# Loading, masking and releasing the attention bias of a head in two halves

## The reference, cut to what matters

```python
scores = einsum('bhqd,bhkd->bhqk', q / sqrt(16), k)      # 8 batches, 16 heads, 512 x 512
scores = scores + attention_bias                         # fp32, 1 MB for one head of one batch
scores = where(src_mask, -inf, scores)                   # the mask is the same for all heads of a batch
probs  = softmax(scores)
ctx    = einsum('bhqk,bhkd->bhqd', probs, v)
```

## Time and profile before

| | |
|---|---|
| time, median of 3 runs | 1041.93 us (1038.78 to 1044.15) |
| profiled execution, span | 1036.6 us (5.3 us under the median; its whole time is not recorded) |
| attention block | first `add_bias` at 39.8 us, last at 706.7 us of the span |
| one batch in the middle | 83.9 to 84.1 us |
| busy over the span | PE 92%, DVE 78%, ACT 71%, POOL 70% |
| bias loads | 128 of 1024 KB, median 8.0 us from issue to landing |

### The profile page before, as it was taken

The page is one execution under the profiler, slowest core; times in us unless marked ns, Lnnn a source line. Parts: engine busy times, 40 slices in busy tenths (PEclk is TensorE's granted clock), DMA queues, the critical chain, the costliest instruction groups (busy, mean ns, idle before and its releaser), DMA issues. The chain is left out here.

```text
span 1036.6 us, 20438 instructions
## 1 busy us (share of the span) xinstructions
PE 956.1 (92%) x5892; PEld 640.9 (62%) x5892; DVE 813.7 (78%) x2075; ACT 734.7 (71%) x1211; POOL 726.3 (70%) x596
## 2 busy tenths in 40 slices
PE   5879999999999999999999999898999999999963
PEld 4646556656655655755665665454777777777752
DVE  8887797878879879879787887874456877887697
ACT  3577887888798788788788878875446556655433
POOL 3487697788788878878778878777555567755631
PEclk9989999999999999999999999999999999999987
DMA  7978978997996997897799799752111111111001
GB/s 262 334 289 292 381 289 278 363 347 238 346 384 214 336 386 257 291 390 292 265 372 343 237 348 370 252 193 82 41 41 41 42 33 50 42 41 41 21 21 41
DMA packets 127535, 230.33 MB, mean 222 GB/s; under 512 B 5488, under 2 KB 53872, under 8 KB 123632
## 3 DMA queue, kind: packets, MB, share of 16 engines
q1 hardware_dynamic: 127472, 229.60, 62.0%
HBM read 187.63 MB, written 41.94 MB: 221 GB/s over the span
## 5 line engine op out<-in xcount | busy, mean ns | idle before, releaser
L937 ACT ACTIVATE prob<-prob,nmax 128x512 f32<-128x512 f32 x512 | 357.0, 729 | 59.6 <-DVE nmax L762 56.4
L762 DVE CUSTOM_DVE_ANT_0 prob<-s_bank,big 128x512 f32<-128x512 f32 x512 | 338.7, 684 | 69.7 <-POOL big L1101 40.3
L1101 POOL TENSOR_TENSOR big<-big,mterm_early 128x2048 f32<-128x2048 f32 (+2 forms) x88 | 305.3, 3484 | 71.5 <-DMA big<-in_fside_Bx16xSxS 62.3
L593 PEld LDWEIGHTS t_bank<-ident,prob 128*128 128x128 f32 x2048 | 238.1, 141 | 168.3 <-issue 51.5
L593 PE MATMUL t_bank<-ident,prob 128*128 128x128 f32 x2048 | 317.7, 278 | 15.9 <-ACT prob L937 6.7
L944 ACT COPY pt<-t_bank 128x512 f32<-128x512 f32 x312 | 181.1, 584 | 51.7 <-PE t_bank L593 50.6
L581 PE MATMUL s_bank<-stack_k,stack_q 128*128 128x512 bf16 x512 | 195.4, 382 | 1.3 <-DVE nmax L762 0.7
L771 DVE COPY pt<-t_bank 128x512 f32<-128x512 f32 x200 | 137.2, 686 | 34.9 <-PE t_bank L593 34.6
L2052 POOL TENSOR_TENSOR gl<-big,gh 128x512 fp32r<-128x512 f32 x64 | 84.6, 1329 | 69.8 <-DVE gh L1643 69.8
L607 PE MATMUL o_bank<-pt,val 128*32 128x512 f32 x1024 | 122.9, 598 | 1.2 <-ACT pt L944 0.7
L1905 ACT ACTIVATE big<-bank,late 128x512 f32<-128x512 f32 x62 | 42.7, 689 | 75.2 <-PE bank L1446 71.4
(11 more groups left out here) (257 smaller groups left out, 1610.0 us busy)
## 6 DMA issues: line engine op xcount, KB each, us to landing
big<-in_fside_Bx16xSxS SPq DMA_DIRECT2D x128, 1024.0 KB, 8.0
pieces_dram<-pieces SPq DMA_DIRECT2D x64, 384.0 KB, 7.3
stack_q<-pieces_dram SPq DMA_DIRECT2D x15, 1024.0 KB, 8.3
stack_k<-pieces_dram SPq DMA_DIRECT2D x15, 1024.0 KB, 10.0
pieces_dram<-pieces SPq DMA_DIRECT2D x32, 256.0 KB, 7.6
xin<-in_x SPq DMA_DIRECT2D x8, 512.0 KB, 8.7
x_dram<-x SPq DMA_DIRECT2D x8, 512.0 KB, 2.6
x1r<-x_dram SPq DMA_DIRECT2D x8, 512.0 KB, 4.3
```

The source lines that it names most:

```text
L593: last = pe.transpose(t_bank[n % 2][:, c * P:(c + 1) * P], prob[:, n % NT, c * P:(c + 1) * P], ident[:])
L762: dve.tensor_tensor_reduce(out=prob[:, n % NT, :], in0=s_bank[n % 3][:, :], in1=bias[:, h % NB, t, :], scale=-1.0, scalar=3e38, op0=ALU.ad ...
L937: act.activation(tile, tile, ACT.Exp, bias=nmax[:, n % NT:n % NT + 1], scale=-1.0).then_inc(exped.sem, 1)
L1101: pool.tensor_tensor(bias[:, h % NB, tiles], bias[:, h % NB, tiles], mterm[:, tiles], ALU.add).then_inc(masked.sem, 1)
```

## The change

Three things:

1. The four tiles of a bias buffer are two halves of two tiles. Each half has a semaphore of its own for its load, is loaded by a DMA of its own (512 KB, 256 runs of 2 KB), is masked by an instruction of its own (two instructions of 1024 elements in place of one of 2048; 1024 and 512 for head 4) and is released by itself: SP waits for `biased` of tiles 0 and 1, loads the first half of head h + 4, waits for tiles 2 and 3, loads the second half.
2. DVE waits at tiles 0 and 2, each time for its half.
3. All `apart` increments of all engines and both blocks go to one semaphore.

The core of the diff (all other lines replace the name of a spacing semaphore, or count halves where heads were counted):

```diff
+HALF = QT // 2
+POOL_HALVES = [(h, i) for h in POOL_HEADS for i in range(2) if POOL_TILES[h] > HALF * i]
+def half_of(i):
+    return slice(HALF * i, HALF * (i + 1))
-        bias_in = [sem(f"bias_in{i}") for i in range(NB)]
+        bias_in = [[sem(f"bias_in{i}{half}") for half in range(2)] for i in range(NB)]
-        first_loads += [(bias[:, h], v["bias"][:, h], bias_in[h]) for h in range(NB)]
+        first_loads += [(bias[:, h, half_of(i)], v["bias"][:, h, half_of(i)], bias_in[h][i]) for h in range(NB) for i in range(2)]
-            def load_bias(b, h):
-                sp.dma_start(bias[:, h % NB], bias_flat[:, bass.ds(b * H + h, 1)].rearrange("p o t k -> p (o t) k")
-                             ).then_inc(bias_in[h % NB], 16)
+            def load_bias(b, h, i):
+                sp.dma_start(bias[:, h % NB, half_of(i)],
+                             bias_flat[:, bass.ds(b * H + h, 1), half_of(i)].rearrange("p o t k -> p (o t) k")
+                             ).then_inc(bias_in[h % NB][i], 16)
                 for h in range(H):
-                    if not (last and h + NB >= H):
-                        sp.wait_ge(biased.sem, biased.at(b, QT * (h + 1)))
-                        apart(sp, sp_apart)
-                        load_bias(b, h + NB)
+                    for i in range(2):
+                        if not (last and h + NB >= H):
+                            sp.wait_ge(biased.sem, biased.at(b, QT * h + HALF * (i + 1)))
+                            apart(sp, k["apart"])
+                            load_bias(b, h + NB, i)
             def add_bias(b, n):
                 h, t = n // QT, n % QT
-                if t == 0 and POOL_TILES[h]:
-                    dve.wait_ge(masked.sem, masked.at(b, POOL_HEADS.index(h) + 1))
-                elif t == 0:
-                    dve.wait_ge(bias_in[h % NB], b * (16 * H // NB) + 16 * (h // NB + 1))
+                i = t // HALF
+                if t % HALF == 0 and (h, i) in POOL_HALVES:
+                    dve.wait_ge(masked.sem, masked.at(b, POOL_HALVES.index((h, i)) + 1))
+                elif t % HALF == 0:
+                    dve.wait_ge(bias_in[h % NB][i], b * (16 * H // NB) + 16 * (h // NB + 1))
             def mask_bias(b, h):
-                pool.wait_ge(bias_in[h % NB], b * (16 * H // NB) + 16 * (h // NB + 1))
...
-                apart(pool, pool_apart)
                 mterm = mterm_early if h < EARLY_HEADS else mterm_late
-                tiles = slice(0, POOL_TILES[h])
-                pool.tensor_tensor(bias[:, h % NB, tiles], bias[:, h % NB, tiles], mterm[:, tiles], ALU.add
-                                   ).then_inc(masked.sem, 1)
+                for i in range(2):
+                    if (h, i) in POOL_HALVES:
+                        pool.wait_ge(bias_in[h % NB][i], b * (16 * H // NB) + 16 * (h // NB + 1))
+                        apart(pool, k["apart"])
+                        tiles = slice(HALF * i, min(HALF * (i + 1), POOL_TILES[h]))
+                        pool.tensor_tensor(bias[:, h % NB, tiles], bias[:, h % NB, tiles], mterm[:, tiles], ALU.add
+                                           ).then_inc(masked.sem, 1)
```

More of the change, by code:

```diff
@@ L350, in attention_block @@
         late_term = Count(sem("late_term"), QT, 0)
-        masked = Count(sem("masked"), len(POOL_HEADS), 0)
+        masked = Count(sem("masked"), len(POOL_HALVES), 0)
         res_done = Count(sem("res_done"), 1, 1)
@@ L1075, in early_mask_term @@
                     if t == 0:
-                        pool.wait_ge(masked.sem, masked.at(b, sum(h < EARLY_HEADS for h in POOL_HEADS)))
-                apart(pool, pool_apart)
+                        pool.wait_ge(masked.sem, masked.at(b, sum(h < EARLY_HEADS for h, _ in POOL_HALVES)))
+                apart(pool, k["apart"])
                 pool.tensor_scalar(
@@ L1084, in late_mask_term @@
                     pool.wait_ge(scored.sem, scored.at(b - 1, STEPS))
-                    pool.wait_ge(masked.sem, masked.at(b - 1, len(POOL_HEADS)))
-                apart(pool, pool_apart)
+                    pool.wait_ge(masked.sem, masked.at(b - 1, len(POOL_HALVES)))
+                apart(pool, k["apart"])
                 pool.tensor_scalar(
@@ L1700, in statistics @@
                 wait(dve, bn_done[i], j, 1)
-                apart(dve, dve_apart)
+                apart(dve, k["apart"])
                 for t in range(QT):
@@ L2160, in build @@
             k[n] = nc.alloc_sbuf_tensor_at(n, [P] + shape, dt, offset=at)
-        for n in ("first_in", "w1_made", "w2_made", "x1_last", "first_made", "mix_step"):
+        for n in ("first_in", "w1_made", "w2_made", "x1_last", "first_made", "mix_step", "apart"):
             k[n] = ctx.enter_context(nc.semaphore(n))
```

17 lines of the change are left out of this document (6 added, 11 removed).

## The result

The changed kernel takes 1050.72 us (median of 4 runs, 1048.93 to 1050.8), the kernel before beside it 1040.77. The ratio is 1.0093, with a 95% interval of 1.0073 to 1.0113: **0.9% slower**, where 0.7% faster was predicted. The profiled executions differ by more than the medians, 1048.7 us of span against 1036.6. (The changed file has 7 or more lines ahead of each place: `add_bias` is now L770, the normalisation L809, the low parts of xt L817, the masks L1111, PE's "XT" L636, "Q" and "K" L644, "W" L669.)

What follows compares the result with a forecast made beforehand. PE was taken to bound the attention block, busy 81.08 of a middle batch's 83.90 us. Gains of 2.8 + 4.8 = 7.6 us off 1041.9 gave 1034.3 us, 0.7% less, range 1027 to 1042.

Steps and rivals of the forecast that it cites:

- The stall is covered by PE's burst: DVE's stall for POOL's masks at head 1: PE fills it with a 1.92 us burst, so first-order gain is nothing.
- Term 1: ACT's copy of "C" before PE's "W": about 0.4 us sooner in 7 batches, 2.8 us, 0 to 5.3.
- Term 2: DVE's normalisation shares less time with POOL's late mask terms: 0.8 us in 6 batches, 4.8 us, 0 to 7.7.
- What the change adds: Extra POOL instructions, SP issues, DVE waits and the single semaphore: 1.4 us of POOL per batch, nothing in the sum.
- Rival C: Bias loads: halves land later, so POOL's masks and late terms slide over the normalisation; 1055 us for 3 us later, chance 0.12.
- Rival A: Stall covered by PE's burst and normalisation still meeting POOL: gain 0 to 5 us, typically 2.8, 1039 us; chance 0.33.
- DVE's wait under 12 us: Sign in the profile after: DVE's whole wait for POOL's masks falls from 40.3 to under 12 us.
- L801 at about 1.9: Sign: the four normalisation instructions on DVE take about 1.9 us in batches 1 to 6, against 2.66 in batch 4.
- PE's wait before "XT" about 0.5 in a batch: Sign: PE's wait for the normalised x falls to about 0.5 us, from 1.25 in batch 4.
- Before "W" 0.35: Sign: PE's wait for the copy of "C" falls to about 0.35 us, from 0.76 in batch 4.
- A batch at 82.6 to 82.8: Sign: a middle batch takes 82.6 to 82.8 us, against 83.90 before.
- It is wrong if PE's gaps move elsewhere: Condition for failure: PE's gaps move to the exponent or a copy of the steps 12 to 16; no size given.

Runs made afterwards that it cites:

- stall given back: Kernel with both waits, but DVE waits at a head's first tile for both half masks, loads and masks still in halves: 1030.93 us, ratio 0.9901.
- both waits: Changed kernel, POOL waiting for DVE's low parts of xt before head 8's masks (all batches but the last) and before the last batch's weight split: 1031.08 us.

## Why the prediction was wrong, point by point

**The stall is covered by PE's burst: right.** The changed kernel is level with before at step 8, and the 10 us of stall given back cost nothing that shows. All but about 0.2 us in a batch was free.

**Term 1, the copy of "C" 0.4 us sooner: wrong, it is 0** (within its bounds of 0 to 5.3). ACT and PE of the changed kernel, as the earlier trace rows:

```profile
387.41 0.59 ACT L952 COPY pt<-t_bank 128x512 f32<-128x512 f32 x1 [1.12 <-PE t_bank L600]
...
392.09 0.60 PE L664 MATMUL spare<-ident,con 128*128 128x128 f32 x4
...
393.35 0.62 ACT L984 COPY cont<-spare 128x512 f32<-128x512 f32 x1
394.10 1.12 PE L669 MATMUL spare<-cont,wo 128*128 128x512 f32 x2 [0.76 <-ACT cont L984]
```

ACT did lose its idle 1.33 us before the exponent, but spent the lead waiting 1.12 us for a transpose of PE, behind the burst. From the end of "C" (392.69) to its copy are 0.66 us, exactly as before (389.89 to 390.55). The failed reading is that ACT's queue was replayed with fixed durations and without the work of PE that it waits for. A lead of one engine is lost here at the first thing that it needs from another.

**Term 2, the normalisation freed of the late terms: right in mechanism, too small.** 0.8 us was taken; it was the full 1.28 of the bound in batches 1 and 3 to 6 of the changed kernel (1.38 us each, 2.05 in batch 2). The mis-sized piece is how much sooner the late terms start. The prediction took 1.2 to 2.0 us, from a mask of head 5 that still waits for its second half. In the changed kernel's batch 4 that half had landed, the four half masks before the late terms run without a gap, and the late terms start 18.60 us after the batch's first `add_bias` in place of 21.81, 3.2 us sooner. What the term is worth shows where nothing collides: with both waits batch 4 is 1.45 us under the 83.90 of before, 1.28 of it the normalisation and about 0.2 the stall. The whole sum was 7.6 us; the kernel with both waits has 9.7 by the medians and 7.6 by the profiled spans.

**"What the change adds": the step that failed.** The cost of POOL's masks was taken from their number and length, set against POOL's idle time, and the only reader thought of was DVE's `add_bias`. That POOL also *starts earlier* was used for the normalisation, where it helps, and for nothing else. The low parts, 10 us further on, were never costed: a term put at nothing without a reason. Yet the earlier trace rows held the mechanism, and the idle 2.61 us of POOL at 409.99 was in the same timeline. The new term is 1.9 us in each of batches 1 to 6, 0.5 to 1.7 in batch 0, and 7.5 in the last. With it the sum is 1034.3 + 6 x 1.9 + 7.5 and those 0.5 to 1.7, 1053.7 to 1054.9, against the 1050.7 measured; term 1, which came to nothing, is 2.8 of the difference.

The Trainium skill has this rule in the section that the prediction cited for the other line (SBUF — State Buffer, Who interferes with whom): a DVE instruction with two SBUF inputs contends with a GpSimd one that reads SBUF, and the later one blocks. The low parts are such an instruction, and the traces agree: 1.56 and 2.62 us long beside masks, 1.28 for both alone. `add_bias`, which reads one input from PSUM, stays at 0.68 to 0.69 us beside masks (407.42 in the changed kernel), which agrees too.

**Rival C, slower by halves that land late: right in sign only.** The halves land sooner: 6.1 us from issue to landing against 8.0, and with whole masks, where POOL needs both halves, head 8's mask of batch 4 starts 31.9 us after the batch's first `add_bias`, before 35.3. The 315 GB/s of a middle batch against 318 are the same bytes in a longer batch; with both waits it is 322. It was the earliness that cost. The Trainium skill's figures, at least 1 MiB in a DMA and about 2 us of fixed cost for each (DMA: Bandwidth & Descriptors, Measured and Two cost components), would have put a price on smaller transfers; the traces here show no such loss at 512 KB.

```profile
big<-in_fside_Bx16xSxS SPq DMA_DIRECT2D x256, 512.0 KB, 6.1
```

**Rival A, hidden: half right.** The stall was covered, as it said, but the normalisation no longer met POOL's late terms (1.38 us), and it had no way to a slower kernel either.

**The signs named for the profile after.** DVE's wait under 12 us: 3.1. L801 at about 1.9: 1.38. PE's wait before "XT" about 0.5 in a batch: 0 in five of seven. Before "W" 0.35: 0.76. A batch at 82.6 to 82.8: 84.27, but 82.45 once the collision is gone. "It is wrong if PE's gaps move elsewhere" is what happened, though not to the steps 12 to 16 that were named, but to steps 22 to 24.

Open is the start: the first `add_bias` lies 0.85 us later in the changed kernel, but anywhere from 39.4 to 42.7 us in the kernels here, without a pattern that goes with the change. Why the kernel with loads whole has three batches of 84.8 to 86.1 us, and the kernel with one semaphore one of 86.0, was not followed up either.

## What to carry to other kernels

When a change makes an engine that shares something with another one *earlier*, go through everything that the other does in the stretch into which the work moves, not only its readers: an idle gap that costs nothing may be the slot in which somebody else runs. Where the two meet on a critical stretch, either order them with one wait on the engine that has time (1.4 us of POOL bought 1.8 us of the batch), or cut the long instruction. Such a wait pays only if nobody waits for what comes behind it, and it has to be checked in the first and the last round of a loop, where the work that it waits for can stand elsewhere.

## What the hardware showed that was not expected

- How sharp the turn-taking is: in one execution the same three instructions give 2.04 or 5.89 us of low parts, and a batch of 82.46 or 88.94, by whether POOL's mask starts before or after the second low part. The runs of that kernel spread over 16 us; that the same accident of order spreads them is likely, but only one of them was traced.
- The same idle time of PE did not always have the same clock behind it. In the kernel with whole masks a wait of 3.36 us in batch 1 left the granted clock at 1.00, and one of 3.35 us in batch 3 had 6.8 us at half the clock beside it, which made the batch 3.0 us longer again. The waits of 1.56 us in the changed kernel had none, its wait of 6.30 us had 6.8 us at half clock, so that 5.6 us more in the low parts became 7.5 us in the last batch.
- Transfers of 512 KB in place of 1024 KB, twice as many: no loss of rate (322 GB/s over a middle batch with both waits, 318 before), and the issues of SP cost nothing that a kernel showed.
